# Two-layer graph network on one core: VectorE adds a group's gathered rows before it adds the preceding group's sums

## What is computed

```python
N, E = 6250, 206250                       # src, dst: (E,), dst ascending
h = jnp.maximum(_layernorm(x, axis=-1), 0.0)
msg = jax.nn.relu(jnp.concatenate([h[src], edge_attr_64], -1) @ W1 + b1) @ W2 + b2
agg = jax.ops.segment_sum(msg, dst, num_segments=N)
g = jax.nn.relu(jnp.concatenate([h, agg], -1) @ U1 + c1)
x = x + g @ U2 + c2
h = jnp.maximum(_layernorm(x, axis=-1), 0.0)
x = x + jax.ops.segment_sum(h[src] * edge_weight[:, None], dst, num_segments=N)
```

## Time and profile before

| what | value |
|---|---|
| time, median of 3 runs | 3135.02 us (3133.75 to 3136.86) |
| profiled execution, its own time | 3122.63 us |
| span of its instructions | 3120.8 us, 49909 instructions |
| mean granted TensorE clock | 0.812 |
| busy: PE, DVE, ACT, POOL | 72%, 52%, 27%, 50% |

### The profile page before, as it was taken

The page is one execution under the profiler, slowest core; times in us unless marked ns, Lnnn a source line. Parts: engine busy times, 40 slices in busy tenths (PEclk is TensorE's granted clock), DMA queues, the critical chain, the costliest instruction groups (busy, mean ns, idle before and its releaser), DMA issues.

```text
span 3120.8 us, 49909 instructions
## 1 busy us (share of the span) xinstructions
PE 2232.2 (72%) x18336; PEld 1691.8 (54%) x18336; DVE 1629.2 (52%) x4964; ACT 849.5 (27%) x1500; POOL 1560.8 (50%) x1635
## 2 busy tenths in 40 slices
PE   4475755666666677677777777777777777777799
PEld 4354544444444455555555555555555655665577
DVE  4445755555555555555554555545555455554455
ACT  4122433222222222222222222223222322222221
POOL 4635255555555545555555455555555544554400
PEclk9867877777777777777777877888888889888899
DMA  4123444433543454355435543553555356525688
GB/s 89 34 91 133 167 135 154 156 129 121 178 137 118 131 186 149 93 167 166 138 108 164 169 132 119 162 170 114 166 166 154 102 160 181 176 78 155 177 275 289
DMA packets 376799, 459.49 MB, mean 147 GB/s; under 512 B 78474, under 2 KB 298890, under 8 KB 372968
## 3 DMA queue, kind: packets, MB, share of 16 engines
q1 hardware_dynamic: 317914, 401.54, 39.4%
q0 software_dynamic: 51712, 53.06, 7.8%
q10 hardware_dynamic: 6926, 1.63, 0.2%
HBM read 281.50 MB, written 174.54 MB: 146 GB/s over the span
## 4 chain that ended last, share of the span: by engine, by line
PE 51%; issue 16%; another core or an unknown queue 15%; DVE 13%; DMA 2%; ACT 1%; SPq 1%; DVEq 0%; ACTq 0%
PE pair L1303 17%; PE pair L1318 9%; PE pair L1342 7%; PE pair L1243 5%; DVE bld L1818 4%; DVE bld L1828 4%; PE pair L1290 3%; PE pair L1349 2%; PE pair L1236 2%; PE pair L1446 1%; DVE rings L1772 1%; PE pair L1376 1%; DMA late_piece<-adjacency 1%; DVE bld L1821 1%
## 5 line engine op out<-in xcount | busy, mean ns | idle before, releaser
L835 POOL DMA_INDIRECT rows<-table,idx x1464 | 1402.6, 958 | 1245.6 <-DVE rings L1772 851.5
L1009 ACT COPY stage<-pair 128x600 f32<-128x600 f32 x808 | 527.8, 666 | 1760.0 <-remote 767.0
L1818 DVE TENSOR_SCALAR bld<-iota_key,key 128x300 bf16<-128x300 f16 x1616 | 536.8, 332 | 798.8 <-remote 509.7
L1303 PE MATMUL pair<-bld 128*128 128x300 bf16 x4848 | 839.1, 328 | 91.8 <-issue 54.1
L1303 PEld LDWEIGHTS pair<-bld 128*128 128x128 bf16 x4848 | 566.1, 122 | 322.3 <-issue 160.4
L1318 PE MATMUL pair<-stage,h 125*64 125x96 f32 x4230 | 380.0, 310 | 191.2 <-issue 188.8
L1828 DVE TENSOR_TENSOR bld<-bld,part 128x512 bf16<-128x512 bf16 x1212 | 490.7, 405 | 0.0
L1318 PEld LDWEIGHTS pair<-stage,h 125*64 125x64 f32 x4230 | 301.6, 179 | 241.5 <-issue 240.8
L1243 PE MATMUL pair<-w1b,rings 128*128 128x128 f32 x1584 | 264.4, 321 | 164.5 <-DVE rings L1772 160.8
L1243 PEld LDWEIGHTS pair<-w1b,rings 128*128 128x128 f32 x1584 | 244.5, 233 | 185.3 <-DVE rings L1772 176.5
L1342 PE MATMUL pair<-late_piece,h 125*64 125x384 f32 (+1 forms) x1040 | 266.5, 642 | 92.9 <-issue 76.8
(11 more groups left out here) (178 smaller groups left out, 1439.1 us busy)
## 6 DMA issues: line engine op xcount, KB each, us to landing
late_piece<-adjacency SPq DMA_DIRECT2D x232, 480.0 KB
rings<-in_edge_attr_dram SPq DMA_DIRECT2D x202, 256.0 KB
adjacency<-stage SPq DMA_DIRECT2D x14, 2160.0 KB
tail<-stage SPq DMA_DIRECT2D x101, 240.0 KB
stage<-tail SPq DMA_DIRECT2D x50, 480.0 KB, 5.9
rows<-table,idx POOLq DMA_INDIRECT x1464
adjacency<-stage SPq DMA_DIRECT2D x10, 1920.0 KB
adjacency<-stage SPq DMA_DIRECT2D x10, 1680.0 KB
```

Of the source, the lines that this page charges most:

```text
L835: pool.indirect_dma_start(out=to[:, t, :], out_offset=None, in_=table, in_offset=bass.IndirectOffsetOnAxis(ap=idx[:, g, t:t + 1], axis=0), ...
L1009: act.copy(tiles[:, g % STAGE, :, 2 * j * WT:2 * (j + 1) * WT].rearrange("p h (o w) -> p o h w", w=WT), build_pair[i % 2][:, :, 0:KEYS].re ...
L1303: last = pe.matmul(build_pair[i // 2 % 2][:, t % 2, 0:KEYS], hot_w[q % 2][k][:, :, u], hot_key[q % 2][:, u, :], start=(k == 0), stop=(k == ...
L1818: return dve.tensor_scalar(hot_key[q % 2][:, u, :], iota_key[:, :], key[:, g, t + u:t + u + 1], None, ALU.is_equal)
```

## The change

In DVE's loop, and there alone, `add_fast(s)` is put ahead of `add_sums(s - 1)`. Nothing is added or removed, and no wait is changed: each instruction keeps the semaphore it waits for.

```diff
                 for s in range(GROUPS):
+                    if s < GROUPS:
+                        add_fast(s)
                     if 1 <= s <= GROUPS:
                         add_sums(s - 1)
                     if s < GROUPS:
-                        add_fast(s)
                         make_hot(s)
```

## The result

| what | before | changed | ratio, 95% interval |
|---|---|---|---|
| time, median of 4 runs | 3134.39 us | 3220.82 us (3217.12 to 3225.90) | 1.028, 1.0257 to 1.0302 |
| profiled execution, its own time | 3122.63 us | 3217.12 us | |
| its span | 3120.8 us | 3215.3 us | |
| mean granted TensorE clock | 0.812 | 0.809 | |

The change makes the kernel 2.8% slower. The forecast was slower, 3184 us: the side is right, the size is 37 us too small. The profiled execution of before, 3122.63 us, is faster than each of the three runs behind its first median (3133.75 to 3136.86) and so isn't one of them; between the two profiled executions the change costs 94.5 us, between the medians 86.4.

A forecast was written before the change was run, and what follows sets the result against it. Taken as the bound: the loop of L1772 counting pre_made, POOL's gathers, PE's results coming out, DVE finishing. Terms -51 + 25 + 66 + 9 = +49 us on 3122.63 gave 3172, plus 12.4 to the median: 3184 us; range 3068 to 3290.

The forecast's parts named there:

- Early steps: 70 steps where DVE waits at L1806 for the preceding group's sums; predicted to pair into double bursts, +66 us.
- late-quad steps: 115 steps where DVE waits at L1818 for a quad; L1772 0.44 us sooner, -51 us, against +25 for later acc_added.
- The lock: Inferred: PE's results pass freely in the first half of POOL's gather burst, then only once it is over.
- rival 1: Gathers don't hold PE up; early steps fall to POOL's own pace, 10.0 us; 2874 us in all; chance 0.08.
- The sum for a pair: Two early steps: gathers 20.30, release 2.00 later, two quads 4.37, next burst 0.96 later; 27.63 us, taken as 27.9.
- The upper bound, 29.28: Pair of early steps if group_done stays locked to the burst's end, adding 1.65 us; +114 us over 70 steps.
- the 1.16 us: In late-quad steps PE's first four tiles come 0.72 later, the burst starts 0.44 sooner: 1.16 us deeper in it.
- Chunk updates: L1376 and L1386 on PE wait for acc_added, counted up to 0.72 us later, at 12 waits: +9 us.
- 2, the leak: Inside a double burst PE gets far enough that only one quad is left afterwards; 3073 us; chance 0.20.
- 3's mechanism: The 1.16 us push first four tiles of half the late-quad steps into the lock: +125 us, 3284; chance 0.16.
- four signs named beforehand: Gather runs of 16 with some 8 us rest; longer L1818 waits, up to 12; L1806 wait behind L1772; clock not rising.
- sign of being wrong: Early steps below 12.7 us, POOL's runs staying at 8, or late-quad steps falling by more than 0.44 us.

The follow-up runs named there:

- wait_first: Changed kernel, but DVE waits for group_done of group s - 1 ahead of add_fast(s): 3064.18 us (0.9921) on first-kind chip; 2238.59 (1.0023), 2239.60 (1.0031) on second.

## Why the prediction was right, and where it was off

**The mechanism** held. Early steps merged in pairs, late-quad steps got shorter, and the clock stayed (0.812, 0.809). The lock, inferred from coincidence in the earlier trace rows, is confirmed as an effect of the gathers: on chips of the first kind half the gathers give 9.3 us a step where all of them took 14.4, and holding the burst back undoes the loss. The sentence from the Trainium skill, SBUF — State Buffer, section "Who interferes with whom", that PE and ACT never wait on anyone, isn't borne out for PE on those chips; on the second kind it fits what is seen, and rival 1's pace came there.

**Early steps: the term that was mis-sized.** Forecast +66 us, measured +92.2 for the 52 in pairs, and +14.7 for early steps that stayed single. The sum for a pair was 20.30 + 2.00 + 4.37 + 0.96 = 27.63, raised to 27.9. The pair above has 19.88 (953.25 to 973.13) + 3.09 + 5.89 + 0.96 = 29.82. Two terms failed. The release came 3.09 us after the last gather instead of 2.00. And the two quads took 976.22 to 982.11, 5.89 instead of 4.37, because the last four tiles of the group weren't built: PE stood 8.30 us at L1303 for ACT's copies, which waited for the locked results. I took the earlier trace rows as the model, near the lower bound; there the one-hot matrix had been made inside the burst. The upper bound, 29.28, was the better choice and still 0.5 short. That its total, +114 us, is near the +115.8 of all 72 steps is chance: it had 70 steps in pairs and nothing for single ones.

**Steps that were early and didn't merge** weren't in the sum. Nineteen of them went from 13.18 to 13.96 us, +14.7; the other 8.9 us of the 23.6 are step 22, a merged one. In step 145, for one, before had the second quad ready 10.5 us into the burst. In the changed kernel the tiles start some 1 us deeper in it, the second pair of them falls behind the lock, and that quad ends at 13.3. This is the 1.16 us that I had laid at the door of late-quad steps. I had taken all 70 early steps to go in pairs.

**Late-quad steps.** -51 and +25 gave -26; measured were 66 steps and -20.4 together, -0.31 each where I had taken 0.44 less a loss. I had counted 115 waits; of the steps behind them only some 66 are of the plain kind with 14.73 us. The loss that I took for half of them doesn't show as such: few of their first quads fell behind the lock.

**Chunk updates**, +9: the 35 steps of over 15 us, in which these lie, rose by 3.5 us together.

**From the sum to the median.** The sum was +49 us, and from one profiled execution to the other it measured +94.5, nearly twice as much. I then added the 12.4 us by which before's median lies above its profiled execution. In the changed kernel that distance is 3.7 us. So some 9 us of the miss are made good by luck, and 37 us are left.

**Rivals.** 1 is refuted on the chips of this kind. 2, the leak, appears inside longer bursts (L1806 was released at 970.51, during the gathers), but no quad was finished by it. 3's mechanism exists, in other steps and at about an eighth of its price. Of the four signs named beforehand, three came: runs of 16, with a rest of 9.9 us instead of 8 behind the one shown, the wait at L1806 behind L1772, and a clock that didn't rise. One didn't: the waits ahead of L1818 didn't grow in length (4.13 us each for 4.43), though there are 135 for 115. The long wait is at L1806, and it hides theirs. No sign of being wrong came: late-quad steps fell by less than 0.44, and merged steps stayed just below 15.

## What to carry to other kernels

A count that is given earlier isn't a gain by itself: ask which queue it lets loose, and whether the other engines need the pause that the old order gave. Here an earlier `pre_made` let POOL's transfers run on over the moment at which PE's results came out; giving the count early and holding the queue back by the event that the others wait for won the loss back, and 0.4% more. And a trace that shows a lock by coincidence is worth an experiment on more than one chip before the order of a kernel is tuned to it.

## What the runs showed of the hardware

The same program took 3085 to 3135 us on one kind of chip and 2233 on the other, a factor of 1.4, each with a spread of at most 0.7% within one comparison. Chip 8 was of the first kind both times, with 3129 and 3088 us for the kernel before. Whether it is the chip or how it is run can't be told from here.

On the first kind, while POOL issues indirect DMAs, PE starts some 115 to 136 instructions at its own pace and then one or a few in 0.7 us, and its semaphores come late: the segment sums of the double burst were started at 957.76 and seen at 970.51. Apart from these sums, what was held back in the steps shown came free 1.6 to 3.1 us after the last gather. DVE's semaphores don't share this. In the changed kernel a burst starts at 501.84, and PE takes up L1243 as soon as L1772, from 508.48 to 509.17, is done:

```profile
508.48 0.69 DVE L1772 TENSOR_TENSOR rings<-rows,pair 128x512 f32<-128x512 f32 x1
...
509.22 1.16 PE L1243 MATMUL pair<-w1b,rings 128*128 128x128 f32 x8 [1.69 <-DVE rings L1772]
```

What the limited thing is wasn't found.

The variant `wait_first` is 0.8% faster than before on the first kind and 0.2 to 0.3% slower on the second; no version was found that is better on both.
